# Rows for the experts scattered in the attention stage and loaded plainly, instead of gathered by index

## The reference

```
x = x + xattn(layernorm(x), ctx)
h = layernorm(x).reshape(T, 512)
probs = softmax(h @ gate_w.T); rw, sel = top_k(probs, 2); rw = rw / rw.sum(-1)
# for each expert e, with cap = ceil(T / 12 * 1.25) = 854:
#   its assignments in the order (first choices of all tokens, then second choices),
#   the first 854 of them kept, tok = token, w = rw or 0 where there are fewer
xs = h[tok]
out[tok] += (silu(xs @ w1[e].T * (xs @ w3[e].T)) @ w2[e].T) * w
x = x + out
```

## Time and profile before

| | us |
|---|---|
| median of 3 runs | 2409.75 |
| profiled execution, own time | 2416.92 |
| its span | 2415.2 |

### The profile page before, as it was taken

How to read it: one execution, slowest core, us unless ns; L and a number is a source line. 1 busy time by engine, 2 the same in 40 slices (tenths; PEclk the granted TensorE clock), 3 DMA queues, 4 the chain that set the end, 5 groups by cost and what they waited for, 6 DMA issues and landing times. The chain is left out here.

```text
span 2415.2 us, 54028 instructions
## 1 busy us (share of the span) xinstructions
PE 2254.9 (93%) x13058; PEld 1145.1 (47%) x13058; DVE 1876.5 (78%) x5286; ACT 1774.2 (73%) x6911; POOL 1096.9 (45%) x1943
## 2 busy tenths in 40 slices
PE   3899999999999999999999999999999999577992
PEld 1345555555555555555555555555555555244550
DVE  5878888888888888888888888888888887545662
ACT  5878788888888888788888888888788887334541
POOL 4434444444444444444444444444444443368875
PEclk9899999999999999999999999999999999878985
DMA  8577766677766777667677767777766776369997
GB/s 252 101 158 145 142 140 140 138 139 143 147 140 143 143 144 141 141 140 140 138 139 143 148 139 143 143 141 142 143 140 140 138 140 126 79 163 189 188 171 94
DMA packets 892480, 347.98 MB, mean 144 GB/s; under 512 B 827115, under 2 KB 827371, under 8 KB 892399
## 3 DMA queue, kind: packets, MB, share of 16 engines
q1 hardware_dynamic: 865822, 296.93, 60.9%
q0 software_dynamic: 22912, 43.15, 9.8%
q10 hardware_dynamic: 3696, 7.34, 0.9%
HBM read 91.20 MB, written 57.63 MB: 62 GB/s over the span
## 5 line engine op out<-in xcount | busy, mean ns | idle before, releaser
L753 PE MATMUL pb<-wo,o 128*128 128x512 f16 x3072 | 711.0, 381 | 15.5 <-DVE o L1011 13.6
L885 ACT ACTIVATE work<-pb,small 128x128 f32<-128x128 f32 x1024 | 455.2, 453 | 174.8 <-DVE small L1074 174.0
L1345 POOL TENSOR_TENSOR small<-small 128x4 f32<-128x4 f32 (+1 forms) x584 | 485.8, 835 | 54.0 <-POOL small L1416 13.8
L1416 POOL TENSOR_TENSOR small<-small 128x4 f32<-128x4 f32 x256 | 84.2, 329 | 878.1 <-ACT junk_q L866 878.1
L753 PEld LDWEIGHTS pb<-wo,o 128*128 128x128 f16 x3072 | 287.2, 98 | 348.3 <-DVE o L1011 18.2
L684 PE MATMUL pb<-wq,xT 128*128 128x512 f16 x1536 | 356.6, 382 | 1.0 <-DVE q L1062 1.0
L684 PE MATMUL pb<-wq,wkv_raw 128*128 128x512 f16 x1536 | 352.4, 379 | 0.7 <-DVE q L1062 0.7
L1062 DVE SCALAR_TENSOR_TENSOR q<-pb,small,q 128x128 f16<-128x128 f32 x1024 | 288.3, 344 | 73.6 <-ACT q L875 73.5
L875 ACT ACTIVATE q<-pb,small 128x128 f16<-128x128 f32 x1024 | 291.1, 366 | 7.2 <-DMA qT<-q 7.2
L866 ACT ACTIVATE junk_q<-pb 128x128 bf16<-128x128 f32 x1024 | 273.4, 305 | 6.7 <-PE pb L684 6.6
L899 ACT ACTIVATE o<-pb 128x512 f16<-128x512 f32 x256 | 153.6, 600 | 138.6 <-PE pb L741 133.3
(11 more groups left out here) (154 smaller groups left out, 3481.8 us busy)
## 6 DMA issues: line engine op xcount, KB each, us to landing
work<-x SPq DMA_DIRECT2D x128, 256.0 KB, 3.1
work<-c SPq DMA_DIRECT2D x64, 256.0 KB, 3.9
out<-work SPq DMA_DIRECT2D x64, 256.0 KB, 2.0
xn_scratch<-work SPq DMA_DIRECT2D x64, 256.0 KB, 2.3
wo_raw<-wo ACTq DMA_DIRECT2D x4, 1024.0 KB, 9.2
qT<-q SPq DMA_TRANSPOSE x256
pT<-p SPq DMA_TRANSPOSE x256
wq_raw<-wq ACTq DMA_DIRECT2D x3, 1024.0 KB, 11.3
```

Source lines behind the costliest of these rows:

```text
L753: mm = nc.tensor.matmul(WO_B[:, :], o16[:, HPG * a + h, :], part(O0 + g, b_)[:, h, :], start=(g == 0 and h == 0 and n == 0), stop=(g == NG ...
L885: ex = nc.scalar.activation(probs[:, cols], S_B[:, cols], ACT.Exp, bias=nmax[:, h:h + 1], scale=esc, accum_out=psums[:, h:h + 1])
L1345: return nc.gpsimd.tensor_tensor(out_, in_, neghalf[:, 0:n], ALU.pow)
```

## The change

Each block's normalised rows are written by POOL, in the attention stage, straight to the places of the token's two experts in a DRAM tensor of 12 x 896 rows (`rows_d`); the tensor xn2_d and its store are gone. `norm2` writes into a tile of its own (`xn2`, two of them) instead of `x_res`. In the expert stage SP loads an expert's 896 rows with one plain DMA (128 partitions, 7 rows of 2 KB in a row each) into one of four buffers, and POOL only issues scatter_adds. The 42 unused places of each expert are filled once at the start with rows of x. Places that no token takes can hold anything, so DVE bounds the loaded rows to -32 to 32 (`bound_rows`) before PE reads them; their weight is 0. The lists are loaded in full, 128 partitions. `HALF` keeps its values (0, 512) and (512, 896).

```diff
+H0 = (NT + 1) // 2
+ROW_MAX = 32.0
 (experts)
+        xg = xg + [sb(f"xg_{i}", [128, NT, HID])[:, :, :] for i in (2, 3)]
+        NX = len(xg)
-        d_g = [[sem(f"d_gathered{i}_{t}") for t in range(NT)] for i in range(2)]
+        d_g = [sem(f"d_rows_{n}") for n in range(NX)]
+        cl_done = sem("rows_bounded")
 (sync)
+            def load_rows(e):
+                wait(sp, tr_done, NT * (e - NX + 1))
+                sp.dma_start(xg[e % NX], rows_d[e * CP:(e + 1) * CP, :].rearrange(
+                    "(p t) n -> p t n", t=NT)).then_inc(d_g[e % NX], 16)
+            sp.wait_ge(s_rows, 32 * NB)
+            for e in range(NX):
+                load_rows(e)
             for e in range(2, E):
                 wait_apart(sp, (h_done, 2 * (e - 1)))
                 sp.dma_start(w13_s[i], w13[e]).then_inc(d_w13[i], 16)
+                if e + 2 >= NX and e + 2 < E:
+                    load_rows(e + 2)
 (gpsimd)
-            pool.wait_ge(s_z, 2)
-            for e in range(3):
-                gather(e // 2, e % 2)
...
-            gather(PAIRS - 1, 1)
-            for e in range(E - 4, E):
-                scatter_add(e // 2, e % 2)
+            for e in range(E):
+                scatter_add(e)
 (tensor, transposes)
+                pe.wait_ge(cl_done, e + 1)
                 for t in range(NT):
-                    pe.wait_ge(d_g[i][t], 16 * (j + 1))
 (vector)
+            def bound_rows(e):
+                dve.wait_ge(d_g[e % NX], 16 * (e // NX + 1))
+                nc.vector.tensor_scalar(xg[e % NX], xg[e % NX], -ROW_MAX, ROW_MAX, ALU.max,
+                                        ALU.min).then_inc(cl_done, 1)
             def step(j, i, more=True):
+                if 2 * j + i + 2 < E:
+                    bound_rows(2 * j + i + 2)
                 if more:
                     products(j + i, 1 - i)
...
+            bound_rows(0)
+            bound_rows(1)
             products(0, 0)
 (build)
-    xn2_d = nc.dram_tensor("xn2_scratch", (T, HID), f32, kind="Internal").ap()
+    rows_d = nc.dram_tensor("expert_rows", (ROWS, HID), f32, kind="Internal").ap()
+        xn2 = [wkv_raw[:, 1, i, :] for i in range(2)]
 (load_res)
-                    wait_apart(sp, (n_lo, b), (d_xn2, 16 * b))
+                    wait_apart(sp, (xn2_done, b), (d_x1, 16 * b))
-                def store_xn2(b):
-                    wait_apart(sp, (xn2_done, b + 1))
-                    sp.dma_start(xn2_d[bass.ds(b * 128, 128), :], x_res).then_inc(d_xn2, 16)
 (load_lists)
+                    sp.dma_start(lists[:, lo:hi, :, :].rearrange("p e t o -> p e (t o)"),
+                                 table_d[lo * CP:hi * CP, :].rearrange("(e p t) o -> p e (t o)", p=128, t=NT)).then_inc(d_lists[i], 16)
 (fill_tables)
+                    pads = CP - CAP
+                    sp.dma_start(rows_d.rearrange("(e r) n -> e r n", r=CP)[:, CAP:CP, :],
+                                 x.rearrange("b t n -> (b t) n")[0:E * pads, :].rearrange(
+                                     "(e r) n -> e r n", r=pads)).then_inc(d_sent, 16)
 (norm2)
-                    wait(dve, d_x1, 16 * (b + 1))
-                    nc.vector.tensor_scalar(x_res, x_res, mv_2[:, 0:1], rstd_2, ALU.subtract,
+                    wait(dve, s_rows, 32 * (b - 1))
+                    nc.vector.tensor_scalar(xn2[par], x_res, mv_2[:, 0:1], rstd_2, ALU.subtract,
                                             ALU.mult).then_inc(xn2_done, 1)
 (place)
                     wait(dve, s_table, 32 * b)
+                    wait(dve, s_rows, 32 * b)
 (gpsimd, attention)
+                def scatter_rows(b, par):
+                    wait_apart(pool, (dst_rdy, b + 1), (n_lo, b + 1), (s_rows, 32 * b))
+                    for k in range(2):
+                        nc.gpsimd.indirect_dma_start(
+                            out=rows_d, out_offset=bass.IndirectOffsetOnAxis(ap=dst[:, k:k + 1], axis=0),
+                            in_=xn2[par], in_offset=None, bounds_check=ROWS - 1,
+                            oob_is_err=False).then_inc(s_rows, 16)
                         if live(far[0]):
                             rms_q(*far)
-                        if isinstance(b, int) and (b, g) in ((NB - 1, 3), (NB, 1)):
-                            nc.gpsimd.memset(xg[0 if b < NB else 1], 0.0).then_inc(s_z, 1)
+                        if g == 1 and live(b - 3):
+                            scatter_rows(b - 3, 1 - par)
```

More of the change, by code:

```diff
@@ L35, in experts @@
     ACT = mybir.ActivationFunctionType
-    wait, wait_apart, sem, pb, ident, xn2_d, s_z, d_lists, d_w13, d_w2, xg, w13_s, w2_s, lists = (gt[k] for k in (
-        "wait", "wait_apart", "sem", "pb", "ident", "xn2_d", "s_z", "d_lists", "d_w13", "d_w2", "xg", "w13_s", "w2_s",
+    wait, wait_apart, sem, pb, ident, rows_d, s_rows, d_lists, d_w13, d_w2, xg, w13_s, w2_s, lists = (gt[k] for k in (
+        "wait", "wait_apart", "sem", "pb", "ident", "rows_d", "s_rows", "d_lists", "d_w13", "d_w2", "xg", "w13_s", "w2_s",
         "lists"))
@@ L83, in _, with scatter_add @@
         def _(pool):
[L84 to L95, removed]
+            def scatter_add(e):
+                j, i = e // 2, e % 2
+                lists_in(pool, e)
                 wait_apart(pool, (d_add[1 - i], 16 * NT * (j + i)))
@@ L159, in down @@
                     cols = slice(t * 128, (t + 1) * 128)
-                    pe.wait_ge(hl_done, 2 * e + (1 if cols.stop <= 512 else 2))
+                    pe.wait_ge(hl_done, 2 * e + (1 if t < H0 else 2))
                     nc.tensor.matmul(Y_B[t % 3][:, :], h_parts[:, cols], w2_hi[:, :], start=True, stop=False)
@@ L356, in build @@
         pb = [psum(f"pb{i}") for i in range(8)]
-        s_table, s_const, s_z, lists_set = (sem(n) for n in ("s_table_scattered", "s_const", "xg_zeroed", "lists_set"))
+        s_table, s_const, s_rows = (sem(n) for n in ("s_table_scattered", "s_const", "s_rows_scattered"))
         d_lists = [sem(f"d_lists_{i}") for i in range(3)]
@@ L1311, in body @@
                         if g == 3 and live(b - 1):
-                            norm2(b - 1)
+                            norm2(b - 1, 1 - par)
                         if g == 3 and live(b + 2):
@@ L1511, in body @@
                         if g == 0 and isinstance(b, int) and b == 2:
-                            pool.wait_ge(d_sent, 32)
-                            pool.wait_ge(w_lo, NC * len(SPLIT))
-                            nc.gpsimd.memset(lists[:, :, :, 1], 0)
-                            nc.gpsimd.iota(lists[:, :, :, 0], pattern=[[0, E], [1, NT]], base=T,
-                                           channel_multiplier=NT).then_inc(lists_set, 1)
+                            pool.wait_ge(d_sent, 48)
                         if g == 1 and live(b - 3):
@@ L1538, in body @@
                             rms_q(*far)
-                        if isinstance(b, int) and (b, g) in ((NB - 1, 3), (NB, 1)):
-                            nc.gpsimd.memset(xg[0 if b < NB else 1], 0.0).then_inc(s_z, 1)
+                        if g == 1 and live(b - 3):
+                            scatter_rows(b - 3, 1 - par)
                 loop(pool, body)
                 pool.wait_ge(s_table, 32 * NB)
-        experts(nc, gt=dict(wait=wait, wait_apart=wait_apart, sem=sem, pb=pb, ident=ident, xn2_d=xn2_d, s_z=s_z,
+                pool.wait_ge(s_rows, 32 * NB)
+        experts(nc, gt=dict(wait=wait, wait_apart=wait_apart, sem=sem, pb=pb, ident=ident, rows_d=rows_d, s_rows=s_rows,
                             d_lists=d_lists, d_w13=d_w13, d_w2=d_w2, xg=xg, w13_s=w13_s, w2_s=w2_s, lists=lists),
```

41 lines of the change are left out of this document (13 added, 28 removed).

## The result

| | before | after |
|---|---|---|
| median of the runs, us | 2409.73 (4 runs, 2409.68 to 2411.4) | 2389.81 (4 runs, 2388.3 to 2393.32) |
| profiled execution, us | 2416.92 | 2388.96 |
| its span, us | 2415.2 | 2387.2 |
| POOL busy in one attention block of 31.4 us | 13.37 | 16.15 |
| first scatter-add S(0), us | 2158.50 | 2152.59 |

The ratio is 0.9918 [0.9901, 0.9935]: faster by 19.9 us, 0.8%. The forecast was 2389.

The account below looks back on a forecast made before the run. POOL's issue was taken to bound the expert stage. Steps of 234.5 falling to 210.8 (-23.7) and a first scatter-add +3.3 later gave -20.4: profiled 2396.5, median 2389 us (own range 2380 to 2398; with rivals 2369 to 2409).

Parts of the forecast that it names:

- POOL's issue as the bound: Expert stage: POOL's issue sets the 22.65 us per expert; without gathers the landing wait leaves 17.7.
- Loaded steps of 20.0: Expert stage: seven steps with a row load take 20.0 us each, halfway between 17.7 and 22.5.
- rival A: Expert stage: the load and scatter-add queues overlap wholly, all 11 steps 17.7 us, 2373 us; chance 0.22.
- rival C: Expert stage: loads starting with a scatter-add delay its landing, loaded cycle 24.5 us, 2421 us, slower; chance 0.12.
- The 22.5 us per cycle: Expert stage: no queue overlap, 21.4 us of DMA work at share 0.95; 2407 us, chance 0.13.
- The hand-over: Attention to expert stage: transposes at 2126, up(0) at 2133, then chain as before; first scatter-add at 2161.8, +3.3 us.
- its offset of 7.2 us: Whole kernel: the median lies 7.2 us under the profiled run, taken as the same after the change.
- Attention: Attention stage: PE-bound blocks stay at 31.4 us, cost 0; DMA share 0.69 to at most 0.72.
- Rival E: Attention stage: 0.3 us more per block gives back 19 us, 2408 us; chance 0.05.
- bound_rows: 2.03 us: DVE, expert stage: each bounding of 128 x 3584 takes 2.0 us, between 1.9 and 2.4.
- rival D: Expert stage: bound_rows and scatter-adds block each other, +2.0 us in 11 steps, 2411 us; chance 0.06.
- Start and tail: Start: pad rows cost 0, at most 3 us; tail from the last expert's first scatter-add: 22.2 us, unchanged.

Follow-up runs that it names:

- e3: Kernel after with odd experts adding to a second tensor, never added to the output, so each waits for the expert two before: 2364.83 us, 0.9791.
- e1: Kernel after without bound_rows on DVE; PE waits for the rows' load directly: 2386.93 us, 0.9872.
- v1: Kernel after with later row loads held until an earlier expert's scatter-adds have landed: 2383.72 us, 0.9895; once more 2382.55 us, 0.9882.
- e4: Kernel before with PE waiting for all seven gathers of expert 0 before its first transpose: one run of 2413.79 us.
- after again: Kernel after once more, without an edit, in a later session: 2391.67 us, 0.9919.
- e5: Kernel after with row loads held by a semaphore behind the seventh scatter-add in POOL's program; most went out 2.9 us behind the first: 2401.41 us, 0.9966.

## Why the prediction was right, and where it was not

**POOL's issue as the bound: right.** The gathers go, a wait takes their place (66.0 us in the 11 brackets ahead of an expert's first scatter-add), and the steps come to 213.1 us for 210.8 forecast. It is the landing wait except in the first step; without it (e3) the brackets are still 43.1 us, waits for outputs then, so the 66.0 are not all to be won.

**Loaded steps of 20.0: the mean right, the mechanism not.** I put them halfway between a full and no overlap of the two queues. The queues overlap fully in e3, which is rival A's premise; rival A's 17.7 fails all the same, because the landing of the scatter-adds is delayed when a load runs beside the last of them, which is rival C's mechanism. C had the moment wrong: it feared loads that go out just when a scatter-add starts, and those that go out just ahead of an expert's first one are the harmless ones. Its price of 24.5 is met in one step of after (24.84; 25.21 once more) and not as the rule, since most loads fall at a good moment. The right split is by the moment: 17.9 to 19.5 for a load that goes out just ahead of the first scatter-add (after, e1 and v1), 20.8 to 22.4 for one 3 to 5.5 us behind it, 23.3 to 25.2 for one between there and the end of the seventh's issue. So a loaded step is worth 18.7 to 22 by where its load is put, and the 20.0 was the mean of both kinds, not a sharing of engines. That the mean came out is luck: where the loads fall follows from the up-projections, which the prediction did not place. The loads also took six steps and not seven, two of them in one step.

The rule in the prediction that all queues share the 16 engines (the Trainium skill, DMA: Bandwidth & Descriptors, "Issuing engines are not separate DMA queues") agrees as to the engines: a landing slows down with another queue's load. The 22.5 us per cycle that the prediction read out of its second half, that a second issuer saves only issue time, were not met: well placed loaded steps took 17.9 to 19.5 us and e3's cycle 16.02 us at a share of 1.06, all shorter than the 21.4 us of the two queues' work one after the other. No run here issues both from one queue, so how much of that is the second queue's doing isn't shown.

**The hand-over: the step that failed.** "Behind it the chain is as before", S(0) +3.3. Measured from the last table scatter, S(0) came after 44.58 us where the kernel before took 49.23: -4.65, a miss of 8, and outside the 2158 to 2167 that the prediction named as a sign of being right. The second pair of traces repeats it (44.11 and 49.34). The stations up to there were right: DVE's bounding ran at 2125.06, and PE:

```profile
2125.06 2.03 DVE L278 TENSOR_SCALAR wq_raw<-wq_raw 128x3584 f32<-128x3584 f32 x1 [19.15 <-DMA wq_raw<-expert_rows]
...
2153.26 1.39 DVE L286 TENSOR_SCALAR yb<-pb,wkv_raw 128x512 f32<-128x512 f32 x2
```

```profile
2127.15 5.08 PE L123 MATMUL pb<-ident,wq_raw 128*128 128x128 f32 x28 [25.41 <-DVE wq_raw L278]
2132.28 6.28 PE L135 MATMUL pb<-xgT,wo_raw 128*128 128x512 f32 x16
...
2141.81 2.12 PE L123 MATMUL pb<-ident,wq_raw 128*128 128x128 f32 x16 [1.94 <-ACT xgT L202]
```

The load was issued at 2116.70 and landed 8.3 us later (8.0 forecast), the transposes were forecast at 2126 and up(0) at 2133. But from up(0) to the first output it is 21.0 us, not the 28.6 that I carried over. I had read that chain only at its ends. It held an up-projection of 8.09 us, the first part of it at half clock, and waits of ACT. In before, e4 and after the granted clock rises between 2128 and 2132, so what starts behind that runs at full clock. Windows of the kernel before and of e4 over the same 4 us:

```profile
2128.00:2132.00 4.00, 4.00 (x7) 1.65 (x6) 0.00 (x0) 0.00 (x0) 3.09 (x4) 0.63 0.71 193
```

```profile
2128.00:2132.00 4.00, 3.70 (x15) 2.49 (x14) 0.00 (x0) 1.75 (x4) 2.67 (x4) 0.85 0.69 193
```

The granted clock is 0.63 in the first and 0.85 in the second, from 0.50 before and to 1.00 behind it in both. Why it rises there wasn't settled. The rest is waits of ACT and what came of them. In the kernel before, ACT starts to copy the second half of h 2.9 us behind the end of up(0), and then waits 2.45 us ahead of expert 1's rows; PE stands idle for 7.34 us, the granted clock is back at 0.50 from 2142 to 2148, and expert 1's last 16 transposes take 3.65 us for 2.12. What ended ACT's waits isn't known; the trace before puts them down to a releaser that it does not name:

```profile
2138.25 0.48 ACT L218 COPY h<-pb 64x384 f32<-64x384 f32 x1 [4.88 <-remote]
...
2143.25 2.44 ACT L211 COPY xgT<-pb 128x512 f32<-128x512 f32 x4 [2.45 <-remote]
```

```profile
2143.98 3.65 PE L131 MATMUL pb<-ident,wq_raw 128*128 128x128 f32 x16 [7.34 <-ACT xgT L211]
```

Added up: 1.8 us for the shorter up(0), 5.4 for ACT's waits and 1.8 for the transposes, less 1.4 us that the chain of after lost again behind up(1), where a bound_rows (2150.25) stands on DVE ahead of the next products. That makes the 7.6.

**Two errors that cancelled, which is luck.** The profiled pair differs by 28.0 us: S(0) -5.9, the steps -21.4, the tail -0.7. The forecast was -20.4 from the profiled run, carried to the median with its offset of 7.2 us. That offset was of the occasion, as far as the runs tell, and not of the profile: the profile after lies 0.9 us under its median, and the kernel before had a median of 2417.09 in another session. With the profiles of before and after taken once more, in two different sessions, the spans differ by 23.1 (S(0) -3.3, steps -19.6, tail -0.2); the medians differ by 18.4 in the session of after again. So S(0) came 9.2 us earlier than forecast in the first pair and 6.6 in the second, the steps gave 2.3 and 4.1 us less, and the profiled difference is larger than that of the medians by 8.1 and 4.7. From the profiled pair the forecast was off by 7.6 us; the occasion's part, which I can't place by line, made it good for the median.

**Attention: right.** In the same window of 31.40 us PE is busy throughout, as before, POOL is busy 16.15 of it, DMA share 0.70 (0.69 to 0.72 forecast). The last table scatter starts no later than in the kernel before (see below). Rival E is out.

**bound_rows: 2.03 us, right; the lock (rival D), half right.** In after it occurs twice and not eleven times: the scatter-add of 2203.20 took 3.39 us beside the bound_rows that DVE began at 2203.15. I had placed bound_rows behind POOL's issue; in two of the steps it slips onto the seventh scatter-add or onto one of the next expert. In after its removal took nothing off the steps, in v1 4.4 us. The Trainium skill (SBUF — State Buffer, "Who interferes with whom") agrees in kind; by its words the blocked engine stands still for the whole instruction, and the 3.39 less 1.54 = 1.85 us of delay is close to DVE's 2.03.

**Start and tail: right.** The last table scatter starts at 2108.01 for 2109.27, and in the second pair at 2108.29 for 2106.39, so start and attention together cost nothing beyond what repeats; the tail is 21.5 us.

## What to carry to other kernels

A chain of read-modify-write transfers that wait for each other's landing is sensitive to when other traffic starts, more than to how much there is: put a prefetch at the moment in which the last group has landed, not as early as its buffer allows. When a bound is taken away, look at what it hid; here a landing wait of some 5 us per expert. A second output tensor took 24.9 us off the steps of after, 17.0 off those of v1, without the adding up of the two, whose price no run shows. And read a chain that you carry over link by link: clock and waits belong to its place in time.

## What the runs showed of the hardware

- Two queues with seven 128-row scatter-adds (14.0 us of 16 engines by the earlier trace rows) and a load of 1.8 MB with weights (7.4 us, an estimate from the earlier trace rows) fitted into 16.02 us, at a share of 1.06.
- A plain load of 1.8 MB in pieces of 14 KB landed in 7.1 to 7.5 us while no scatter-add ran (the load of expert 4), in 7.8 to 9.9 when it went out just ahead of a step's first scatter-add (v1), and in 8.7 to 10.3 when 2.9 us behind it (e5).
- The bracket ahead of an expert's first scatter-add was 4.2 to 6.5 us with no load in the step before it or one that went out just ahead of that step, 7.2 to 10.2 with one 2.9 to 8.5 us into the step, 9.8 to 10.6 with one during the seventh scatter-add's issue, and 4.9 to 6.6 with one just behind that.
- A tensor_scalar of 128 x 3584 fp32 on DVE took 2.03 us and where the two met, a scatter-add on POOL took 2.9 to 3.4 us instead of 1.54.
- The kernel before had medians of 2409.7, 2410.1, 2411.3 and 2417.1 us on four occasions.
